# Where six maximum passes stand among sixteen heads, and when the last feed-forward result is drained

## What is computed

```python
x = x + layernorm(attention(layernorm(x)))          # 16 heads of 32, rotary angles by head, causal softmax
x = x + layernorm(ffn(layernorm(x)))                # two ternary linear layers of 512 to 2048 to 512, gelu between
```

## Time and profile before

| | before |
|---|---|
| median of 3 runs | 1356.84 us (1355.69 to 1360.48) |
| the profiled execution's own time | 1356.18 us |
| its span, first to last instruction | 1354.4 us |
| TensorE busy with matmuls | 1202.9 us, 89% |
| VectorE busy | 1015.4 us, 75% |
| ScalarE busy | 769.4 us, 57% |
| GpSimd busy | 595.7 us, 44% |
| mean granted TensorE clock | 0.948 of full speed |

### The profile page before, as it was taken

How to read it: one execution, slowest core, us unless ns; L and a number is a source line. 1 busy time by engine, 2 the same in 40 slices (tenths; PEclk the granted TensorE clock), 3 DMA queues, 4 the chain that set the end, 5 groups by cost and what they waited for, 6 DMA issues and landing times.

```text
span 1354.4 us, 24946 instructions
## 1 busy us (share of the span) xinstructions
PE 1202.9 (89%) x9364; PEld 655.1 (48%) x9364; DVE 1015.4 (75%) x2931; ACT 769.4 (57%) x1414; POOL 595.7 (44%) x636
## 2 busy tenths in 40 slices
PE   4755879998999999998999999998999999988796
PEld 2322554455545554455545554554545554554352
DVE  7587797977787788967787777967787777777532
ACT  3334773665556664665566664665566655576470
POOL 6131342791149402881159312871159313971252
PEclk9865899999999999999999999999999999989798
DMA  5441121002310113002300212001300221001000
GB/s 202 129 152 64 27 76 56 1 4 54 101 33 2 42 46 102 1 18 58 105 12 2 56 50 83 1 24 50 111 7 3 56 59 44 2 1 55 9 1 32
DMA packets 49825, 65.37 MB, mean 48 GB/s; under 512 B 8581, under 2 KB 33189, under 8 KB 49192
## 3 DMA queue, kind: packets, MB, share of 16 engines
q1 hardware_dynamic: 49704, 63.77, 15.9%
HBM read 29.89 MB, written 8.39 MB: 28 GB/s over the span
## 4 chain that ended last, share of the span: by engine, by line
PE 50%; DVE 33%; ACT 5%; SPq 5%; issue 3%; DMA 2%; POOL 2%; POOLq 0%; DVEq 0%; ACTq 0%
PE gen L488 17%; PE down L531 15%; DVE score L1089 8%; PE score L557 4%; PE score L488 4%; DVE hT L950 4%; PE pv L585 3%; DVE gen L1089 3%; DVE probs L950 2%; SPq L397 2%; PE gen L548 2%; DVE mx L1089 2%; SPq L396 2%; PE score L563 2%; PE gen L483 1%
## 5 line engine op out<-in xcount | busy, mean ns | idle before, releaser
L809 ACT ACTIVATE probs<-score 128x512 f16<-128x512 f32 (+1 forms) x384 | 202.1, 526 | 133.4 <-PE score L557 133.4
L1423 POOL TENSOR_TENSOR rstd<-veps,mhalf 128x1 f32<-128x1 f32 (+1 forms) x104 | 67.4, 648 | 468.3 <-DVE veps L1166 349.9
L531 PE MATMUL down<-t2T,hT 128*128 128x512 f16 x1024 | 236.0, 384 | 13.7 <-DVE xn L1151 13.7
L950 DVE TENSOR_TENSOR probs<-score,probs 128x512 f16<-128x512 f32 (+1 forms) x384 | 213.6, 596 | 45.8 <-ACT score L811 45.1
L488 PE MATMUL gen<-x2T,t1T 128*128 128x512 f16 x1024 | 242.9, 383 | 4.0 <-ACT x2T L752 2.5
L811 ACT ACTIVATE score<-score 128x512 f32<-128x512 f32 (+1 forms) x384 | 205.0, 534 | 0.0
L488 PE MATMUL gen<-xT,wa 128*128 128x512 f16 x768 | 182.7, 390 | 20.9 <-DVE mx L1089 11.9
L1089 DVE CUSTOM_DVE_ANT_0 score<-score,mask_rows 128x512 f32<-128x512 f32 (+1 forms) x344 | 157.8, 521 | 0.0
L531 PEld LDWEIGHTS down<-t2T,hT 128*128 128x128 f16 x1024 | 97.0, 99 | 124.2 <-DVE xn L1151 16.3
L950 DVE TENSOR_TENSOR hT<-gen,hT 128x512 f16<-128x512 f32 x160 | 108.7, 685 | 53.4 <-ACT gen L772 27.5
L488 PEld LDWEIGHTS gen<-x2T,t1T 128*128 128x128 f16 x1024 | 95.4, 98 | 109.6 <-ACT x2T L752 5.2
(11 more groups left out here) (136 smaller groups left out, 1834.5 us busy)
## 6 DMA issues: line engine op xcount, KB each, us to landing
qk<-qkn SPq DMA_DIRECT2D x384, 64.0 KB, 2.0
xo<-x SPq DMA_DIRECT2D x8, 1024.0 KB, 5.3
hT<-x SPq DMA_DIRECT2D x8, 1024.0 KB, 6.5
out<-xn SPq DMA_DIRECT2D x32, 256.0 KB, 2.0
hT<-w_fc SPq DMA_DIRECT2D x4, 1024.0 KB, 6.7
hT<-w_down SPq DMA_DIRECT2D x4, 1024.0 KB, 5.4
hT<-w_attn SPq DMA_DIRECT2D x4, 512.0 KB, 10.2
hT<-w_attn SPq DMA_DIRECT2D x1, 1024.0 KB, 8.7
```

The costliest lines, as they stand in the source:

```text
L531: mm = nc.tensor.matmul(down[:, :], hT[:, half, u, PARTS * tb:PARTS * (tb + 1)], t2T[:, u, :], start=(u == 0 and half == HI), stop=(u == F ...
L809: nc.scalar.activation(probs[:, h % 2, HI, 512 * i:512 * i + n], score[i][:, 0:n], ACT.Exp, scale=1.0 / S_UP)
L950: return V.tensor_tensor(out, whole, hi, ALU.subtract)
```

## The change

Two things are moved; no instruction is added or taken away. `STEP_MAX` puts the six maximum passes of the next batch at heads 8 to 13 in place of 5, 6, 9, 10, 13 and 14. The last block of the feed-forward result (`final(3)`, `final_moments(3)`, `final_terms(3)` on VectorE, `final(3)` on ScalarE) is moved behind the end of the heads: on VectorE behind `o_low(0)` and `o_low(1)`, on ScalarE behind `o_turned(2)`.

```diff
--- before.py
+++ after.py
@@ -74,7 +74,7 @@
 PAIR2_AT = {h: PAIRS + h - 4 for h in range(4, 4 + PAIRS)}
 
 
-STEP_MAX = {5: 0, 6: 1, 9: 2, 10: 3, 13: 4, 14: 5}
+STEP_MAX = {8: 0, 9: 1, 10: 2, 11: 3, 12: 4, 13: 5}
 EARLY = len(STEP_MAX)
 MAX_AT = {0: 6, 2: 7, 3: 8, 5: 9, 7: 10, 8: 11, 9: 12, 10: 13, 11: 14, 12: 15}
 SHIFT_AT = 14
@@ -915,9 +915,9 @@
                         values(0)
                     o_turned(0)
                     o_turned(1)
+                    o_turned(2)
                     if prev:
                         final(3)
-                    o_turned(2)
                     normalise_y(0)
                     o_turned(3)
                     normalise_y(1)
@@ -1309,8 +1309,6 @@
                         if h + 1 < HEADS:
                             probs_low(h + 1)
                         head_output(h)
-                        if prev and h == HEADS - 2:
-                            final(3)
                     if prev and h in FINAL_AT:
                         final_moments(FINAL_AT[h])
                         final_terms(FINAL_AT[h])
@@ -1331,11 +1329,12 @@
                 if here:
                     if nxt:
                         v_low(0)
+                    o_low(0)
+                    o_low(1)
                     if prev:
+                        final(3)
                         final_moments(3)
                         final_terms(3)
-                    o_low(0)
-                    o_low(1)
                     y_moments(0)
                     o_low(2)
                     y_moments(1)
```

## The result

| | before | changed |
|---|---|---|
| median | 1356.26 us (4 runs, 1353.16 to 1360.48) | 1333.89 us (4 runs, 1333.18 to 1335.75) |
| ratio | | 0.9834, 95% interval 0.981 to 0.9859 |
| profiled execution | 1356.18 us, span 1354.4 us | 1333.62 us, span 1331.8 us |
| mean granted TensorE clock | 0.948 | 0.958 |

The kernel before also scatters more: over the 26 timings beside the later experiments it took 1348.45 to 1363.66 us. Its time goes with the clock: the fastest of them had a mean granted clock of 0.958, the slowest 0.944.

A forecast was written before the change was run, and what follows sets the result against it. TensorE's waits bound the heads, VectorE the stretch behind them. Six usual batches (-11.4 us), the last attention (+1.35) and the set-up batch (-0.5) gave -10.55 us, hence 1346 us; the stated range was 1339 to 1353 us.

The forecast's parts named there:

- heads 5 to 7: Two passes leave, so head 7's query product starts 3.69 us earlier in a usual batch.
- head 8: A pass comes in and takes the place of a 0.85 us wait; the down product starts 0.05 us later.
- head 11: A pass comes in at a price: the next product starts 1.51 us later, with ends of 0.55 and 2.4 us.
- head 12: A pass comes in before a down product in its own bank: +0.06 us.
- heads 14 and 15: The pass at head 14 leaves, so the last weighing comes 4.32 us after head 15's scores, not 5.50: -1.18 us.
- behind the heads: The moved last result delays normalise_y(0) and o_low(3) up to the next up stage: +1.35 us, bounds 0 and 2.20.
- The set-up batch's heads: Only the heads' part applies, and VectorE's weight-making takes most back: -0.5 us, between -2.5 and +1.5.
- VectorE bound: Rival: VectorE falls behind in steps 8, 11, 12, adding two 0.85 us waits per usual batch: 1356 us, chance 0.16.
- slower: Rival: the clock falls at the new waits, 13 falls of 1.7 us cost 22 us: 1368 us, chance 0.07.
- six of them by -11.4 us: Six usual batches, each -3.25 us in the heads and +1.35 us behind them, so -1.90 us each.
- the last attention's +1.35 us: The last attention has only the loss from the moved last result: +1.35 us.
- Falls of the clock in usual batches: Rival: less waiting at heads 5 to 7 ends two clock falls, winning 3.4 us more: 1342.6 us, chance 0.12.

The follow-up runs named there:

- experiment 3: Changed kernel, but GpSimd takes the first projected block's power before adding the residual of the last feed-forward block: 1330.6 us, ratio 0.9795.
- experiment 2: Changed kernel with the old pass table (heads 5, 6, 9, 10, 13, 14), so only the drain moves: 1362.5 us, ratio 1.0041.
- experiment 6: Kernel before with passes at heads 6, 8, 9, 10, 13, 14 (head 5's pass moved to head 8): 1344.78 us, ratio 0.9893.
- experiment 7: Kernel before with passes at heads 5, 8, 9, 10, 13, 14 (head 6's pass moved to head 8): 1342.93 us, ratio 0.988.
- experiment 8: Changed kernel with an added TensorE wait at head 7, before the query product, for the first low half of its probabilities: 1355.06 us, ratio 0.997.
- experiment 1: Kernel before with only the passes moved to heads 8 to 13, drain left as before: 1330.99 us, ratio 0.9799.
- experiment 4: Kernel before with passes at heads 8, 9, 10, 12, 13, 14, none at head 11, drain as before: 1328.32 us, ratio 0.978.

## Why the prediction was wrong

**Right, step by step:** heads 5 to 7 (9.47 to 5.78 us, forecast 5.78), head 8 (+0.08 for +0.05), head 11 (+1.54 for +1.51), head 12 (+0.08 for +0.06), heads 14 and 15 (-1.17 for -1.18), behind the heads (+1.23 for +1.35), together -1.93 us for -1.90 us. The mechanism of each, the bank cycle and the queue behind the addition, was shown, the last by experiment 3. The set-up batch's heads changed by -0.6 us for -0.5, but that match is luck: with the passes at 5, 6, 9, 10, 13 and 14 they took 80.7 and 79.7 us (experiment 2), with the passes at 8 to 13 between 80.1 and 81.0 us. The rivals "VectorE bound" and "slower" did not come: in the usual batch shown, the scores behind heads 8, 11 and 12 waited for nothing, and no usual batch of the changed kernel shows a fall of the clock.

**Wrong: the sum "six of them by -11.4 us".** It multiplied one batch by six, and that batch was the cheapest of the kernel before. Two terms were missing in it, a longer wait for DMAs and the clock, and the last attention's +1.35 us was wrong too. Against -10.55 us stand -22.6 us between the two spans:

- *The DMA wait at head 5* was taken at its size in that batch. In batches 1, 5 and 6 it was 1.1, 0.6 and 0.7 us longer: 2.4 us more won. Experiments 6 and 7 show it go and stay with the pass at head 5. Why it is longer in three batches was not found.
- *Falls of the clock in usual batches.* Two at head 7 of the kernel before (1.3 and 1.5 us over the usual 7.41) and one behind the heads of batch 4 (1.47 us) are gone. That is 4.3 us. The forecast saw the two at head 7, gave their going 0.12 of chance and left it out of the likeliest time. Its argument against the mechanism, that the 1.64 us wait caused no fall in most batches, is true of the kernel before (four of six) but does not speak against it. In the four kernels with a wait of 1.5 to 1.8 us at head 7 (before, experiments 2, 6 and 8) the clock fell there in 2, 2, 4 and 4 of six batches; in the six without it (the changed one twice, experiments 1, 3, 4 and 7) in none of 36. TensorE: Matmul & The Clock Gate in the Trainium skill, section on the HAM clock gate, has the default at half rate and activity releasing it; these runs agree in so far as the falls in usual batches all follow a wait of 1.3 to 1.8 us.
- *No fall of the clock*, though it looks like one: in one usual batch of each of the ten profiles the first transpose comes 0.35 us late at full clock, behind 0.46 us of idle VectorE in front of line 1206. It is in batch 4 of the kernel before and in batch 5 of the changed one, so it cancels. TensorE waits equally long in both places; before, the clock fell there (1.88 us for the eight transposes, the 1.47 us above), changed, it did not (1.09 us). Timeline of TensorE, before and changed:

```profile
816.90 1.88 PE L483 MATMUL gen<-ident,xo 128*128 128x128 f32 x8 [1.34 <-DVE xo L1206]
```

```profile
951.25 1.09 PE L483 MATMUL gen<-ident,xo 128*128 128x128 f32 x8 [1.33 <-DVE xo L1206]
```

- *The last attention* took 66.13 us in place of 68.65 us, although nothing in its heads changed but the drain of block 3: -2.5 us. Over the kernels it took 66.1 to 69.9 us, and the mean granted clock of this stretch goes with it, from 0.95 (66.1 us) over 0.90 (67.1) and 0.88 (68.6) to 0.86 (69.9). From its first transpose to the end, +0.2 us in place of +1.35. Busy time of that stretch (columns as in rows 10), before and changed:

```profile
1184.80:1253.45 68.65, 57.73 (x575) 34.47 (x571) 49.18 (x117) 44.56 (x99) 28.20 (x29) 0.88 0.08 28
```

```profile
1164.54:1230.68 66.14, 54.31 (x575) 32.76 (x571) 47.75 (x115) 44.66 (x99) 28.31 (x29) 0.95 0.09 29
```

- 1.1 us of the difference lie before the heads of the set-up batch, where both kernels are alike.

Six usual batches at -3.2 and +1.2 us (-11.8), and -2.4, -4.3, -0.6, -1.1, -2.5 and +0.2 us for the items named (the -0.6 is the set-up batch's heads), are -22.5 us. This account holds for the two profiled executions; the last attention and the -1.1 us are differences that another pair of executions need not repeat.

**What stays open:** why the last attention keeps its clock longer in some kernels. Four profiles with the late drain and GpSimd's addition in front (the changed one twice, experiments 2 and 8) have 66.1 to 67.7 us there, and the kernel before and experiments 1, 3, 4 and 6 have 68.6 to 69.9 us. But experiment 7, which drains as before, has 67.15 us, so the drain alone does not decide it. Open too is which of six equal batches gets a fall at head 7. Nor was it tried why a wait of 1 to 1.5 us at head 5 leaves the clock alone and one of 1.5 us at head 7 does not. The one at head 7 stands right behind the sums of one column (line 519) and a weighing, small matmuls both; that this makes the difference is a guess, and no run moved the wait away from them.

## What to carry to other kernels

Before multiplying the gain of one period by the number of periods, measure all periods between the same two marks: here 81.4 to 83.5 us for the same instructions, and most of the spread was a price of the two waits that the change removed. A wait in front of TensorE costs its own length and can cost the clock behind it: at head 7, 1.3 to 1.7 us on top of 1.5 to 1.8 us in 12 of 24 batches, and nothing on top at head 5. And a piece of work moved into a hole of one engine must fit the holes of every engine that takes it up in turn: the drain fitted VectorE, but its addition on GpSimd then stood in front of a power on the critical chain.

## What the runs showed that was not expected

- The kernel's time scatters with the granted clock. The kernel before took 1348 to 1364 us (clock 0.943 to 0.958), the changed one 1333 to 1336 and 1335 to 1340 us, and experiment 4, 1327 to 1329 us. Which falls make up the scatter can't be read from timings alone.
- A wait of 1.51 us, added at one place in each of six batches, cost 19 us in all.
- The same twelve stacking DMAs kept TensorE waiting 0.4 us in three batches and 1.0 to 1.5 us in three.
